# A linear-attention and mixture-of-experts kernel on one core: the experts work on blocks of 256 tokens instead of 512, one unit is a whole expert, and they start three steps behind the attention instead of five

## The chip, the cores and the metric

The kernel runs on one core of a Trainium2 chip. Its time is the device time of one execution in microseconds (us); three runs of the kernel before gave 826.29 to 827.23, with a median of 827.23. The engines are called PE (TensorE, the matmuls), DVE (VectorE), ACT (ScalarE), POOL (GpSimd) and SP (SyncE, which issues most transfers).

## The reference

The input x has 4096 tokens of 256 channels. Two blocks follow each other, each with a layer norm before it and a residual add behind it.

```python
x = x + attn(layernorm(x), w_qkv, w_out)
x = x + ffn(layernorm(x), Wg, Wu, Wd, Wr, temperature)
# attn: 16 heads of 16; q, k get rope, then elu(. * SCALE) + 1
#   kv += outer(k_t, v_t); ks += k_t                 (causal running sums)
#   out_t = (q_t . kv) / max(q_t . ks, 1e-6);  then out @ w_out
# ffn: inh = sigmoid(x @ Wr / temperature); w from the distance of inh to 1/e,
#   with a fallback to the two nearest experts; normalised over 8 experts
#   out = sum_e w_e * ((silu(x @ Wg_e) * (x @ Wu_e)) @ Wd_e)   (256 -> 256 -> 256)
```

All 8 experts are computed for every token; the router gives only their weights.

## The kernel before

The tokens are cut into 32 tiles of 128. Attention goes tile by tile: `qkv`, rope, `scores` (with a causal mask), `av` (scores times v, plus the running state times q), `state`, then the transpose `o_T`, the output projection `proj`, the second layer norm, the transpose `x2_T` and the router's `logit`. The experts go by blocks of B = 512 tokens, which are 4 tiles. A unit is half an expert (128 of its 256 inner channels) for one block. It is `gate` and `up` (six matmuls each with 512 columns moving, line 394), `silu` (ACT, line 615), `h_up` (DVE, line 988), the split of the product into a high and a low part (`h_hi` on ACT, line 622; `h_lo` on POOL, line 1131), and `down` (twelve matmuls with 256 columns moving, line 427). Behind every second unit four `acc` instructions (DVE, line 1000) add the weighted result to the tile's residual. There are 16 units to a block, 8 blocks and so 128 units.

All matrices are kept as a high and a low part in the fp32r type, so each product takes three matmuls (high x high, low x high, high x low). The expert weights are split at the start too: 24 slabs (Wg, Wu and Wd of 8 experts), each loaded by a transfer into a ring of three buffers, rounded on ACT (`slab_hi`, line 479), and its low part made on POOL or DVE (`slab_lo`, lines 1041 and 696).

The order on every engine is written out by hand, instruction by instruction. Each engine runs its own list strictly in order, and a wait stops all that stands behind it. The lists have a head, and then a loop over steps s. In step s the attention takes tile a = s at its front (`qkv`, `scores`) and tile c = s - 1 at its back (`av` to `x2_T`), and four units n = 4 (s - 5) and up are worked. The number 5 is LAG: no unit starts before four tiles are through the attention, since a block has four tiles. Step 5 is the first of the loop, and the first `gate` stands at its start. Attention ends with step 32; steps 33 to 37 hold experts only. The router (28 small DVE instructions, lines 880 to 981, and three on ACT) works on a whole block and stands in every fourth step. Two kinds of ACT function take turns in a step, which costs table loads (line 615 and line 511).

The PSUM banks: gate and up have one each, `down` writes y0 and y1 (two tiles each), the attention has four.

Of the kernel before, what the change touches and what calls it, by code (L numbers as in the profile page):

```python
# [8 lines left out]
F32R = mybir.dt.float32r  # L9
# [17 lines left out]
UNITS = E * KI  # L27
# [41 lines left out]
def build(nc, x, xT, w_qkv, w_out, Wg, Wu, Wd, Wr, temperature, tab, out):  # L69
# [8 lines left out]
    with ctx:  # L78
# [170 lines left out]
        def tensor_program(pe):  # L249
# [140 lines left out]
            def three(ps, weights, b, e_, m_):  # L390
                n = 0
                for wi, xi in ((0, 0), (1, 0), (0, 1)):
                    for k in range(KD):
                        m = pe.matmul(ps, weights[wi][:, e_, k, m_ * P:(m_ + 1) * P], x2[xi][:, b % 2, k, :],  # L394
                                      start=(n == 0), stop=(n == 3 * KD - 1))
                        n += 1
                return m

            def gate(n):
                if not live_unit(n):  # L400
                    return
                b, u = divmod(n, UNITS)
                w.wait_ge(*slab_lo_done(3 * (u // KI)))
                w.wait_ge(s_x2lo, NT * (b + 1))
                w.wait_ge(s_g, n)
                three(G[:, :], wg_p, b, u // KI, u % KI).then_inc(s_gate, 1)

            def up(n):
                if not live_unit(n):
                    return  # L410
                b, u = divmod(n, UNITS)
                w.wait_ge(*slab_lo_done(3 * (u // KI) + 1))
                w.wait_ge(s_h, n)
                w.wait_ge(s_lg, NT)
                three(U[:, :], wu_p, b, u // KI, u % KI).then_inc(s_up, 1)

            def down(n):
                if not live_unit(n):
                    return
                u = n % UNITS  # L420
                w.wait_ge(*slab_lo_done(3 * (u // KI) + 2))
                w.wait_ge(s_hlo, n + 1)
                for t in range(NT):
                    if n % KI == 0 and t % 2 == 0:
                        w.wait_ge(s_acc, NT * (n // KI) - 2 + t)
# [9 lines left out]
            qkv(0); qkv(1); scores(0, 0); scores(0, 1); qkv(2); av(0); scores(1, 0); state(0); qkv(3); scores(1, 1)  # L435
            o_T(0); proj(0); av(1); scores(2, 0); state(1); x2_T(0); o_T(1); scores(2, 1); qkv(4); proj(1); av(2)
            logit(0); state(2); scores(3, 0); x2_T(1); o_T(2); scores(3, 1); logit(1); proj(2); av(3); x2_T(2)
            o_T(3); state(3); proj(3); scores(4, 0); logit(2); x2_T(3); scores(4, 1); logit(3)
            for s in range(LAG, STEPS):
                a, c, d, n = s, s - 1, s - 2, NT * (s - LAG)  # L440
                if s > LAG:
                    logit(d)
                gate(n); qkv(a); up(n); down(n - 2); av(c); gate(n + 1); up(n + 1); down(n - 1); state(c); o_T(c)
                gate(n + 2); proj(c); up(n + 2); down(n); gate(n + 3); scores(a, 0); x2_T(c); up(n + 3); down(n + 1)
                scores(a, 1)

        def scalar_program(act):
# [14 lines left out]
            def load_slab(n):  # L462
# [5 lines left out]
                elif n:  # L468
# [4 lines left out]
            def slab_hi(n):  # L473
# [6 lines left out]
                load_slab(n + NSL - 1)  # L480
# [94 lines left out]
            def x2_hi(g):  # L575
# [3 lines left out]
                w.wait_ge(s_up, UNITS * (b - 1))  # L579
# [49 lines left out]
            a_hi(1, 0); v_copy(2); exp(2); s1(0); a_hi(1, 1); q_hi(2); k_hi(2); slab_hi(6); s2(0); a_hi(1, 2)
            o_hi(0); a_hi(1, 3); x_hi(4); v1(2); qk_copy(3); v2(2); a_hi(2, 0); v_copy(3); wr_hi(); exp(3); s1(1)  # L630
            x2_hi(0); v1(3); a_hi(2, 1); s2(1); q_hi(3); o_hi(1); a_hi(2, 2); v2(3); x_hi(5); slab_hi(7); a_hi(2, 3)
            k_hi(3); qk_copy(4); slab_hi(8); slab_hi(9); v_copy(4); lg_copy(0); s1(2); a_hi(3, 0); x2_hi(1)
            a_hi(3, 1); o_hi(2); exp(4); a_hi(3, 2); v1(4); s2(2); lg_copy(1); a_hi(3, 3); k_hi(4); q_hi(4); v2(4)
            slab_hi(10); o_hi(3); x2_hi(2); slab_hi(11); s1(3); lg_copy(2); a_hi(4, 0); x2_hi(3); a_hi(4, 1); s2(3)
            lg_copy(3)
            for s in range(LAG, STEPS):
                a, c, d, n = s, s - 1, s - 2, NT * (s - LAG)
                router = (s - LAG) // NT if (s - LAG) % NT == 0 else -1
                if s > LAG:
                    lg_copy(d)  # L640
                a_hi(c, 2); th(router); slab_hi(slab(s, 0)); a_hi(c, 3); x_hi(a + 1); qk_copy(a); silu(n); v_copy(a)
                h_hi(n - 1); slab_hi(slab(s, 1)); e1(router); fb(router); exp(a); silu(n + 1); q_hi(a); k_hi(a)
                o_hi(c); h_hi(n); slab_hi(slab(s, 2)); h_hi(n + 1); silu(n + 2); v1(a); slab_hi(slab(s, 3)); s1(c)
                h_hi(n + 2); x2_hi(c); a_hi(a, 0); silu(n + 3); a_hi(a, 1); v2(a); s2(c)

        def vector_program(v):
# [343 lines left out]
            def acc(n, t):  # L990
# [3 lines left out]
                b, e_ = n // UNITS, n % UNITS // KI  # L994
# [266 lines left out]
```

## Time and profile before

| | us |
|---|---|
| median of three runs | 827.23 |
| the profiled execution | 828.06 |
| its span, first to last instruction | 826.3 |
| PE busy | 779.8 (94%) |
| DVE busy | 621.2 (75%) |
| POOL busy | 524.5 (63%) |
| ACT busy | 479.1 (58%) |
| chain that ended last: PE's share | 87% |

The profiled execution's time stands 1.7 us above its span. A matmul's own duration in the trace is longer than its share of PE, because matmuls overlap; the distance between the starts of two of them is what one costs. "Granted clock" is the TensorE clock as a share of 2.4 GHz, and has two levels, 0.5 and 1.0.

### The profile page before, as it was taken

How to read it: one execution, taken by the hardware profiler on the slowest of the kernel's cores; microseconds unless marked ns; L12 is line 12 of the kernel's file. 1: busy time of each engine (PE TensorE's matmuls, PEld its weight loads, DVE VectorE, ACT ScalarE, POOL GpSimd, SP SyncE). 2: the span in 40 equal slices, each digit the busy share in tenths (PEclk: the TensorE clock that was granted, in tenths of full speed). 3: DMA queues.
4: the chain of work that ended last, by engine and by line, in shares of the span. 5: the costliest groups of instructions: out<-in, count | busy, mean ns of one | idle time of the engine just before them, and what ended most of it. 6: DMA issues, size and time to landing. Idle time of an engine off the chain costs nothing.

```text
span 826.3 us, 18214 instructions
## 1 busy us (share of the span) xinstructions
PE 779.8 (94%) x6728; PEld 666.8 (81%) x6728; DVE 621.2 (75%) x1562; ACT 479.1 (58%) x910; POOL 524.5 (63%) x569
## 2 busy tenths in 40 slices
PE   5466899999999999999999999999999999999997
PEld 3345678888888888888888888888888888888886
DVE  5677787879877897778877898778977798756333
ACT  3564576757666656666656566666665666634222
POOL 2789677866667666666677666666776666653332
PEclk9555699999999999999999999999999999999999
DMA  5433333211111221110211231111212121100000
GB/s 149 111 67 88 76 82 88 53 38 40 39 34 39 41 66 39 34 41 20 53 40 39 42 65 33 39 18 32 65 40 39 40 52 27 22 6 26 1 1 25
DMA packets 97320, 38.27 MB, mean 46 GB/s; under 512 B 74192, under 2 KB 96976, under 8 KB 97232
## 3 DMA queue, kind: packets, MB, share of 16 engines
q1 hardware_dynamic: 90704, 30.83, 17.5%
q10 hardware_dynamic: 6528, 6.29, 2.7%
q8 instruction: 53, 0.87, 0.4%
q14 instruction: 35, 0.29, 0.1%
HBM read 16.13 MB, written 4.19 MB: 25 GB/s over the span
## 4 chain that ended last, share of the span: by engine, by line
PE 87%; POOL 4%; DVE 4%; ACT 2%; issue 1%; DMA 1%; ACTq 0%; SPq 0%; DVEq 0%; POOLq 0%
PE y L427 21%; PE gate L394 21%; PE up L394 20%; PE front L275 5%; PE back L320 3%; PE front L276 3%; PE back L356 2%; PE back L298 2%; PE back L331 2%; POOL a_lo L1103 2%; PE front L370 1%; PE front L383 1%; PE back L313 1%; PE back L343 1%; POOL rop L1074 1%
## 5 line engine op out<-in xcount | busy, mean ns | idle before, releaser
L1131 POOL TENSOR_TENSOR h_lo<-work,h_hi 128x512 fp32r<-128x512 f32 x128 | 165.5, 1297 | 71.1 <-ACT h_hi L622 71.1
L1103 POOL TENSOR_TENSOR a_lo<-am,a_hi 128x512 f16<-128x512 f32 x120 | 141.1, 1189 | 30.6 <-ACT a_hi L551 30.4
L427 PE MATMUL y<-wd_hi,h_hi 128*128 128x256 f32 x512 | 144.1, 281 | 1.1 <-DVE xa L1000 1.1
L427 PE MATMUL y<-wd_lo,h_hi 128*128 128x256 f32 x512 | 145.0, 283 | 0.0
L427 PE MATMUL y<-wd_hi,h_lo 128*128 128x256 f32 x512 | 143.5, 280 | 0.0
L622 ACT ACTIVATE h_hi<-work 128x512 fp32r<-128x512 f32 x128 | 80.9, 632 | 75.6 <-PE y L427 42.8
L1082 POOL TENSOR_TENSOR k_st<-qk,k_st 128x512 f16<-128x512 f32 x32 | 39.9, 1248 | 132.5 <-ACT k_st L527 132.5
L1000 DVE SCALAR_TENSOR_TENSOR xa<-y,wo,xa 128x256 f32<-128x256 f32 x256 | 111.5, 476 | 8.1 <-PE y L427 8.1
L988 DVE TENSOR_TENSOR work<-work,up 128x512 f32<-128x512 f32 x128 | 87.2, 681 | 34.3 <-PE up L394 32.5
L775 DVE TENSOR_TENSOR am<-back,cmask 128x512 f32<-128x512 f32 x112 | 74.5, 685 | 49.4 <-PE back L298 49.4
L427 PEld LDWEIGHTS y<-wd_hi,h_hi 128*128 128x128 f32 x512 | 96.3, 188 | 6.5 <-issue 1.2
L427 PEld LDWEIGHTS y<-wd_lo,h_hi 128*128 128x128 f32 x512 | 96.0, 188 | 5.2
L427 PEld LDWEIGHTS y<-wd_hi,h_lo 128*128 128x128 f32 x512 | 97.2, 190 | 0.0
L615 ACT ACTIVATE work<-gate 128x512 f32<-128x512 f32 x128 | 75.9, 593 | 35.5 <-PE gate L394 31.1
L551 ACT ACTIVATE a_hi<-am 128x512 f16<-128x512 f32 x120 | 75.4, 628 | 35.0 <-DVE am L775 32.5
L394 PE MATMUL gate<-x_hi,wg_hi 128*128 128x512 f32 x256 | 88.0, 425 | 0.1
L394 PE MATMUL up<-x_hi,wu_hi 128*128 128x512 f32 x256 | 82.2, 402 | 0.5 <-DVE work L988 0.4
L394 PE MATMUL gate<-x_hi,wg_lo 128*128 128x512 f32 x256 | 80.7, 396 | 0.0
L394 PE MATMUL up<-x_hi,wu_lo 128*128 128x512 f32 x256 | 79.9, 393 | 0.0
L394 PE MATMUL gate<-x_lo,wg_hi 128*128 128x512 f32 x256 | 79.8, 393 | 0.0
L394 PE MATMUL up<-x_lo,wu_hi 128*128 128x512 f32 x256 | 79.5, 392 | 0.0
L751 DVE SCALAR_TENSOR_TENSOR rop<-rop 128x512 f32<-128x512 f32 x32 | 48.5, 1515 | 19.3 <-POOL rop L1074 19.2
(182 smaller groups left out, 1757.4 us busy)
## 6 DMA issues: line engine op xcount, KB each, us to landing
xr<-xT SPq DMA_DIRECT2D x32, 128.0 KB, 2.1
xa<-x SPq DMA_DIRECT2D x32, 128.0 KB, 2.5
out<-xa SPq DMA_DIRECT2D x32, 128.0 KB, 1.9
xa<-Wg ACTq DMA_DIRECT2D x8, 256.0 KB, 2.8
work<-Wu ACTq DMA_DIRECT2D x8, 256.0 KB, 2.8
work<-Wd ACTq DMA_DIRECT2D x8, 256.0 KB, 3.0
work<-w_qkv SPq DMA_DIRECT2D x2, 384.0 KB, 3.6
qT<-q_st SPq DMA_TRANSPOSE x32, 3.2
```

The costliest lines, as they stand in the source:

```text
L275: pe.matmul(R0[:, :], lhs, wqkv_p[wi][:, k, 0:2 * D], start=first, stop=last)
L394: m = pe.matmul(ps, weights[wi][:, e_, k, m_ * P:(m_ + 1) * P], x2[xi][:, b % 2, k, :], start=(n == 0), stop=(n == 3 * KD - 1))
L427: m = pe.matmul(Y[t // 2][:, t % 2 * D:(t % 2 + 1) * D], h_p[hi][:, n % 2, t * P:(t + 1) * P], wd_p[wi][:, u // KI, u % KI, :], start=(n % ...
L551: act.activation(a_p[0][:, heads(r), :], am_place(g, r).rearrange("p (h n) -> p h n", h=4), ACT.Copy).then_inc(s_ahi, 1)
L615: act.activation(hb[:, n % 2, :], G[:, :], ACT.Silu).then_inc(s_g, 1)
L622: act.activation(h_p[0][:, n % 2, :], hb[:, n % 2, :], ACT.Copy).then_inc(s_hhi, 1)
L751: v.scalar_tensor_tensor(out=rop[:, :], in0=rop[:, :], scalar=1.0, in1=rop2[:, :], op0=ALU.add, op1=ALU.add).then_inc(s_rope, 1)
L775: v.tensor_tensor(am_place(g, r).rearrange("p (h n) -> p h n", h=4), score_bank(g, r)[:, :].rearrange("p (h n) -> p h n", h=4), bcast(cmas ...
L988: v.tensor_tensor(hb[:, n % 2, :], hb[:, n % 2, :], U[:, :], ALU.mult).then_inc(s_h, 1)
L1000: v.scalar_tensor_tensor(out=xs, in0=Y[t // 2][:, t % 2 * D:(t % 2 + 1) * D], scalar=wo[:, b % 2, t, e_:e_ + 1], in1=xs, op0=ALU.mult, op1 ...
L1103: pool.tensor_tensor(a_p[1][:, heads(r), :], am_place(g, r).rearrange("p (h n) -> p h n", h=4), a_p[0][:, heads(r), :], ALU.subtract).then ...
L1131: pool.tensor_tensor(h_p[1][:, n % 2, :], hb[:, n % 2, :], h_p[0][:, n % 2, :].bitcast(F32), ALU.subtract).then_inc(s_hlo, 1)
```

## The change

- B goes from 512 to 256, so a block has two tiles and there are 16 blocks. A unit is a whole expert for two tiles; a block has 8 units, and the whole still has 128, four to a step.
- `gate` and `up` write both halves of the expert into one bank: twelve matmuls with 256 columns moving, instead of six with 512. `down` keeps its twelve, and alternates between y0 and y1 from unit to unit. Two `acc` follow every unit, instead of four every second.
- The router stands in every second step instead of every fourth, and works on two tiles.
- LAG goes from 5 to 3. The loop still starts with s = 5 (FULL), but now with unit 8: units 0 to 7 are woven into the written-out head, and all 24 slabs are split there, through a ring of six buffers, alternately on POOL and DVE. Steps 33 to 35 hold experts only.
- All five lists are written in a new order.

```diff
-B = 512
+B = 256
-UNITS = E * KI
+BW = KI * B
+UPS = E // NT
-LAG = 5
+LAG = 3
+FULL = LAG + 2
-NSL = 3
+NSL = 6
...
-            def three(ps, weights, b, e_, m_):
-                n = 0
-                for wi, xi in ((0, 0), (1, 0), (0, 1)):
-                    for k in range(KD):
-                        m = pe.matmul(ps, weights[wi][:, e_, k, m_ * P:(m_ + 1) * P], x2[xi][:, b % 2, k, :],
...
+            def both_halves(ps, weights, b, e_):
+
+                for m_ in range(KI):
+                    for wi, xi in ((0, 0), (1, 0), (0, 1)):
+                        for k in range(KD):
+                            m = pe.matmul(ps[:, m_ * B:(m_ + 1) * B], weights[wi][:, e_, k, m_ * P:(m_ + 1) * P],
+                                          x2[xi][:, b % 2, k, :], start=(m_ == 0 and k == 0 and (wi, xi) == (0, 0)),
...
             def down(n):
...
+                w.wait_ge(s_acc, NT * (n - 1))
                 for t in range(NT):
...
+                    for m_ in range(KI):
+                        tok = slice(m_ * B + t * P, m_ * B + (t + 1) * P)
+                        for wi, hi in ((0, 0), (1, 0), (0, 1)):
+                            m = pe.matmul(Y[n % 2][:, t * D:(t + 1) * D], h_p[hi][:, n % 2, tok], wd_p[wi][:, e_, m_, :],
...
-            for s in range(LAG, STEPS):
-                a, c, d, n = s, s - 1, s - 2, NT * (s - LAG)
-                if s > LAG:
-                    logit(d)
-                gate(n); qkv(a); up(n); down(n - 2); av(c); gate(n + 1); up(n + 1); down(n - 1); state(c); o_T(c)
-                gate(n + 2); proj(c); up(n + 2); down(n); gate(n + 3); scores(a, 0); x2_T(c); up(n + 3); down(n + 1)
-                scores(a, 1)
+            for s in range(FULL, STEPS):
+                a, c, d, n = s, s - 1, s - 2, UPS * (s - LAG)
+                logit(d); gate(n); up(n); qkv(a); down(n - 2); av(c); down(n - 1); gate(n + 1); up(n + 1); o_T(c)
+                state(c); gate(n + 2); proj(c); up(n + 2); down(n); gate(n + 3); up(n + 3); scores(a, 0); x2_T(c)
+                down(n + 1); scores(a, 1)
```

Three places show what moved. The first is PE in the head, around the first gate matmul. Before, it stands behind the scores of tile 4 (`back<-qT,kT`) and the last logits of the first block (`up<-wr_s`), and the qkv of tile 5 follows.

```order
L370 MATMUL up<-ident,nat 128x128 x2
L298 MATMUL back<-qT,kT 128x128 x8
L383 MATMUL up<-wr_s,x_hi 128x16 x2
L386 MATMUL up<-wr_s,x_lo 128x8 x2
L394 MATMUL gate<-x_hi,wg_hi 128x512 x2
L394 MATMUL gate<-x_hi,wg_lo 128x512 x2
L394 MATMUL gate<-x_lo,wg_hi 128x512 x2
L275 MATMUL front<-wqkv_hi,xo_hi 128x512
```

Now it stands behind the scores of tile 2, and gate and up are made of pieces with 256 columns.

```order
L293 MATMUL back<-qT,kT 128x128 x8
L365 MATMUL up<-ident,nat 128x128 x2
L378 MATMUL up<-wr_s,x_hi 128x16 x2
L381 MATMUL up<-wr_s,x_lo 128x8 x2
L293 MATMUL back<-qT,kT 128x128 x8
L390 MATMUL gate<-x_hi,wg_hi 128x256 x2
L390 MATMUL gate<-x_hi,wg_lo 128x256 x2
L390 MATMUL gate<-x_lo,wg_hi 128x256 x2
L390 MATMUL gate<-x_hi,wg_hi 128x256 x2
```

The first unit comes two tiles earlier. The second place is PE in a step of the loop, from the end of `av` (`back<-vx,a_lo`) on. Before, gate and up follow, then (left out behind the last row) `down`, `state` and `o_T`.

```order
L320 MATMUL back<-vx,a_lo 128x51
L394 MATMUL gate<-x_hi,wg_hi 128x512 x2
L394 MATMUL gate<-x_hi,wg_lo 128x512 x2
L394 MATMUL gate<-x_lo,wg_hi 128x512 x2
L394 MATMUL up<-x_hi,wu_hi 128x512 x2
L394 MATMUL up<-x_hi,wu_lo 128x512 x2
L394 MATMUL up<-x_lo,wu_hi 128x512 x2
```

Now `down`, gate and up follow `av`, and the rows from that up on are these, with `o_T` (`back<-ident,nat`) ahead of `state` (`back<-vx,k_st`).

```order
L390 MATMUL up<-x_hi,wu_hi 128x256 x2
L390 MATMUL up<-x_hi,wu_lo 128x256 x2
L390 MATMUL up<-x_lo,wu_hi 128x256 x2
L390 MATMUL up<-x_hi,wu_hi 128x256 x2
L390 MATMUL up<-x_hi,wu_lo 128x256 x2
L390 MATMUL up<-x_lo,wu_hi 128x256 x2
L338 MATMUL back<-ident,nat 128x128 x2
L326 MATMUL back<-vx,k_st 128x34 x24
L390 MATMUL gate<-x_hi,wg_hi 128x256 x2
```

`state` no longer stands between `down` and `o_T`. The third place is DVE in a step with a router, from the denominators (`den`) to the normed output that `o_T` waits for (`nat<-osb,rec`). Before:

```order
L805 TENSOR_SCALAR den<-osb 128x16
L917 SCALAR_TENSOR_TENSOR r_c<-r_eq,iota 128x32
L920 TENSOR_REDUCE q_ws<-r_w 128x4
L922 TENSOR_REDUCE q_ix<-r_c 128x4
L924 TENSOR_SCALAR q_no<-q_ws 128x4
L759 SCALAR_TENSOR_TENSOR qk<-rop 128x512
L930 TENSOR_TENSOR r_s<-iota,q_ix 128x32
L932 SCALAR_TENSOR_TENSOR r_nd<-r_s,r_dist 128x32
L935 TENSOR_REDUCE q_m<-r_nd 128x4
L937 TENSOR_TENSOR r_fw<-r_fb,q_no 128x32
L811 RECIPROCAL rec<-den 128x16
L943 TENSOR_TENSOR r_eq<-r_nd,q_m 128x32
```

Now:

```order
L801 TENSOR_SCALAR den<-osb 128x16
L699 TENSOR_TENSOR xo_lo<-xr,xo_hi 128x256
L755 SCALAR_TENSOR_TENSOR qk<-rop 128x512
L807 RECIPROCAL rec<-den 128x16
L913 SCALAR_TENSOR_TENSOR r_c<-r_eq,iota 128x16
L916 TENSOR_REDUCE q_ws<-r_w 128x2
L918 TENSOR_REDUCE q_ix<-r_c 128x2
L920 TENSOR_SCALAR q_no<-q_ws 128x2
L815 SCALAR_TENSOR_TENSOR nat<-osb,rec 128x256
```

Four of the router's instructions stand between the reciprocal and the normed output now, and the split of the next x tile (`xo_lo`) has come in ahead of them; six of the router's (four before `rec`, and two between it and `nat`) have gone behind `nat`.

## Rows read from the trace of the kernel before

**Rows 1.** The page's slices: busy tenths, and the granted clock.
```profile
PE   5466899999999999999999999999999999999997
...
PEclk9555699999999999999999999999999999999999
```

**Rows 2.** Stretches: length, busy time of PE, PEld, DVE, ACT, POOL, clock, DMA.
```profile
20.00:92.40 72.40, 44.66 (x472) 34.83 (x471) 52.35 (x120) 38.39 (x84) 57.40 (x61) 0.57 0.41 92
92.40:135.00 42.60, 40.25 (x346) 33.18 (x347) 35.95 (x95) 30.84 (x57) 30.21 (x31) 0.96 0.29 74
212.70:588.60 375.90, 375.90 (x3362) 324.81 (x3362) 303.10 (x769) 235.65 (x444) 248.35 (x273) 1.00 0.19 41
```

**Rows 3.** PE in order of time, first gate: start, us, line, operation.
```profile
92.40 1.20 PE L394 MATMUL gate<-x_hi,wg_hi 128*128 128x512 f32 x2
...
95.11 0.63 PE L275 MATMUL front<-wqkv_hi,xo_hi 128*128 128x512 f32 x1
```

**Rows 4.** PE in order of time, one unit behind the attention's end.
```profile
761.74 0.28 PE L427 MATMUL y<-wd_hi,h_hi 128*128 128x256 f32 x1
...
763.17 0.62 PE L394 MATMUL gate<-x_hi,wg_hi 128*128 128x512 f32 x2
...
764.56 0.62 PE L394 MATMUL up<-x_hi,wu_hi 128*128 128x512 f32 x2
...
765.94 0.28 PE L427 MATMUL y<-wd_hi,h_hi 128*128 128x256 f32 x1
```

**Rows 5.** PE in order of time, `proj` and the `up` behind it.
```profile
321.12 0.40 PE L356 MATMUL back<-wout_hi,ox_hi 128*128 128x256 f32 x2
...
321.82 0.62 PE L394 MATMUL up<-x_hi,wu_hi 128*128 128x512 f32 x2
```

**Rows 6.** PE, the first gate of two steps that follow each other.
```profile
306.96 0.72 PE L394 MATMUL gate<-x_hi,wg_hi 128*128 128x512 f32 x2
...
330.44 0.71 PE L394 MATMUL gate<-x_hi,wg_hi 128*128 128x512 f32 x2
```

**Rows 7.** DVE in order of time, head: `x1_add` and `x2_lo` of tile 1.
```profile
65.16 0.43 DVE L834 TENSOR_TENSOR xa<-y,xa 128x256 f32<-128x256 f32 x1 [3.07 <-PE y L356]
...
73.85 0.41 DVE L872 TENSOR_TENSOR x_lo<-up,x_hi 128x256 fp32r<-128x256 f32 x1
```

**Rows 8.** Groups from 212.7 to 588.6 us: count, busy, mean ns, idle before.
```profile
L1000 DVE SCALAR_TENSOR_TENSOR xa<-y,wo,xa 128x256 f32<-128x256 f32 x128 | 56.2, 476 | 0.0
L988 DVE TENSOR_TENSOR work<-work,up 128x512 f32<-128x512 f32 x64 | 43.5, 680 | 0.0
...
L917 DVE SCALAR_TENSOR_TENSOR r_c<-r_eq,iota 128x32 f32<-128x32 f32 x4 | 0.7, 182 | 0.0
...
L615 ACT ACT_TABLE_LOAD x16 | 20.5, 1283 | 10.9 <-PE gate L394 10.9
...
L1131 POOL TENSOR_TENSOR h_lo<-work,h_hi 128x512 fp32r<-128x512 f32 x64 | 82.1, 1287 | 8.9 <-ACT h_hi L622 8.9
```

**Rows 9.** One `slab_lo` on DVE and one on POOL, in order of time.
```profile
28.52 0.68 DVE L696 TENSOR_TENSOR wd_lo<-work,wd_hi 128x512 fp32r<-128x512 f32 x1
...
37.52 1.28 POOL L1041 TENSOR_TENSOR wg_lo<-xa,wg_hi 128x512 fp32r<-128x512 f32 x1
```

**Rows 10.** PE, the gate behind `av`: a step with a router, one without.
```profile
291.00 0.71 PE L394 MATMUL gate<-x_hi,wg_hi 128*128 128x512 f32 x2
...
314.57 0.71 PE L394 MATMUL gate<-x_hi,wg_hi 128*128 128x512 f32 x2
```

**Rows 11.** DVE, the normed output in both, and rope in the second.
```profile
295.19 0.42 DVE L819 SCALAR_TENSOR_TENSOR nat<-osb,rec 128x256 f32<-128x256 f32 x1
...
313.17 1.66 DVE L751 SCALAR_TENSOR_TENSOR rop<-rop 128x512 f32<-128x512 f32 x1 [0.65 <-POOL rop L1074]
...
317.49 0.42 DVE L819 SCALAR_TENSOR_TENSOR nat<-osb,rec 128x256 f32<-128x256 f32 x1
```

**Rows 12.** DVE, the last `acc` instructions.
```profile
822.14 1.66 DVE L1000 SCALAR_TENSOR_TENSOR xa<-y,wo,xa 128x256 f32<-128x256 f32 x4 [2.52 <-PE y L427]
```

More of the change, by code:

```diff
@@ L431, in down @@
                 m.then_inc(s_down, 1)
             colmean()
[L435 to L438, printed above, removed]
@@ new lines, in tensor_program @@
+            proj(0); av(1); state(1); x2_T(0); o_T(1); logit(0); proj(1); qkv(3); scores(2, 0); x2_T(1); logit(1)
+            scores(2, 1); gate(0); up(0); av(2); gate(1); up(1); gate(2); state(2); o_T(2); up(2); proj(2); down(0)
+            gate(3); down(1); up(3); x2_T(2); scores(3, 0); gate(4); logit(2); scores(3, 1); qkv(4); up(4); down(2)
+            gate(5); av(3); up(5); down(3); state(3); gate(6); o_T(3); down(4); proj(3); up(6); gate(7)
+            scores(4, 0); up(7); x2_T(3); down(5); scores(4, 1)
@@ L629, in scalar_program @@
[L629 to L637, printed above, removed]
-                router = (s - LAG) // NT if (s - LAG) % NT == 0 else -1
[L639 to L644, printed above, removed]
+            x_hi(0); load_slab(0); load_slab(1); load_slab(2); load_slab(3); wqkv_hi(0); wqkv_hi(1)
@@ L1020, in vector_program @@
[L1020 to L1031 removed]
+            tcos_scale(0); bn(3); wout_lo(); rtemp_half(); cos(0); rope(0); x_lo(1); x_lo(2); phi(0); slab_lo(1)
@@ new lines, in vector_program @@
+            mean_var2(2); var_eps2(2); slab_lo(15); bn(5); route_both(0); x_lo(4); ln2(2); tcos_scale(4)
+            route_out(0); mask(3, 0); x2_lo(2); mask(3, 1); acc(0, 0); h_up(3); slab_lo(17); mask(3, 2); slab_lo(19)
+            acc(0, 1); acc(1, 0); mask(3, 3); acc(1, 1); h_up(4); cos(4); rope(4); o_sum(3, 0); phi(4); acc(2, 0)
+            o_sum(3, 1); den_max(3); den_rec(3); acc(2, 1); norm(3); x_lo(5); q_lo(4); mean_var(5); acc(3, 0)
+            var_eps(5); o_lo(3); h_up(5); st_add(3); acc(3, 1); x1_add(3); acc(4, 0); slab_lo(21); bn2(3); h_up(6)
@@ new lines, in vector_program @@
+            mean_var2(3); var_eps2(3); mask(4, 0); ln2(3); acc(4, 1); mask(4, 1); h_up(7); x2_lo(3); slab_lo(23)
+            for s in range(FULL, STEPS):
+                a, c, d, n = s, s - 1, s - 2, UPS * (s - LAG)
+                router = (s - LAG) // NT if (s - LAG) % NT == 0 else -1
+                mask(c, 2); acc(n - 3, 0); acc(n - 3, 1); bn(a + 1); mask(c, 3); mean_var(a + 1); h_up(n)
+                route_sum(router); tcos_scale(a); route_zone(router); cos(a); route_nearest(router); var_eps(a + 1)
+                acc(n - 2, 0); o_sum(c, 0); rope(a); o_sum(c, 1); route_weight(router); den_max(c); x_lo(a + 1)
+                phi(a); den_rec(c); route_first(router); norm(c); route_second(router); q_lo(a); o_lo(c)
+                h_up(n + 1); acc(n - 2, 1); acc(n - 1, 0); route_tie(router); route_ix2(router); st_add(c)
+                route_s2(router); x1_add(c); route_both(router); bn2(c); h_up(n + 2); mean_var2(c); var_eps2(c)
+                acc(n - 1, 1); route_out(router); ln2(c); acc(n, 0); mask(a, 0); mask(a, 1); x2_lo(c); acc(n, 1)
+                h_up(n + 3)
@@ new lines, in gpsimd_program @@
+            a_lo(3, 0); a_lo(3, 1); a_lo(3, 2); sin(4, 1); sin(4, 0); a_lo(3, 3); h_lo(3); slab_lo(18); h_lo(4)
+            k_lo(4); slab_lo(20); slab_lo(22); st_rest(3); v_rest(4); h_lo(5); rstd2_pow(3); rstd1_pow(5); s3(3)
+            h_lo(6); v3(4); a_lo(4, 0); a_lo(4, 1)
+            for s in range(FULL, STEPS):
+                a, c, n = s, s - 1, UPS * (s - LAG)
+                h_lo(n - 1); a_lo(c, 2); a_lo(c, 3); sin(a, 1); sin(a, 0); v_rest(a); h_lo(n); k_lo(a); h_lo(n + 1)
+                st_rest(c); rstd2_pow(c); rstd1_pow(a + 1); v3(a); h_lo(n + 2); s3(c); a_lo(a, 0); a_lo(a, 1)
@@ L1207, in sync_program @@
             load_xr(0); load_xa(0); load_xr(1)
-            for g in range(1, NT):
+            for g in range(1, AHEAD + 1):
                 load_xa(g)
```

150 lines of the change are left out of this document (68 added, 82 removed).

## The prediction

> **What bounds the kernel now.** I read the slices first. PE is at 9 tenths from the sixth slice to the last but one; only the first five, about 100 us, show it at 4 to 8 tenths and its clock at half [rows 1]. The stretches say it sharper: from 212.7 to 588.6 us PE is busy for all 375.9 us at clock 1.00, while DVE has 303.1, POOL 248.4 and ACT 235.7; from 20 to 92.4 us PE is busy for only 44.7 of 72.4 us, at a mean clock of 0.57 [rows 2]. So there are two regimes. In the loop the kernel is as long as its matmuls, and only a change in what PE has to do, or a new wait of PE, moves the time. In the head, PE waits for the chain of one tile after the other, and whatever PE work is put there is cheap.
>
> Then the order of time on PE. The first gate starts at 92.40 [rows 3]. A step of the loop takes 330.44 - 306.96 = 23.48 us [rows 6]. A unit costs 765.94 - 761.74 = 4.20 us: 1.43 for `down`, 1.39 for gate, 1.38 for up [rows 4]. Four units are 16.8 us, so the attention's share of a step is 6.7 us. All of PE's work at the full clock is 128 x 4.20 + 32 x 6.7 = 752 us. The span is 826.3; the 74 us between are the head's loss, but for some 11 behind 92.4.
>
> **The split of gate and up: +6 us (+4 to +12).** 256 matmul groups (128 gates, 128 ups) change from 6 x 512 to 12 x 256 columns; that is 3072 columns each time, but 1536 more matmuls in all. The nearest rows with 256 columns are two. `down` is twelve of them in 1.43 us, against (1.39 + 1.38) / 2 = 1.385 for six of 512 [rows 4]: 0.045 x 256 = +11.5 us. `proj` is six of them in 321.82 - 321.12 = 0.70 us [rows 5], so twelve in 1.40: 0.015 x 256 = +3.8 us. Both are of the same type with a new stationary operand each time. Which is nearer is open: gate is like `proj` in that activations that were ready long ago are read, like `down` in its number. I take +6, nearer to `proj`, and keep both ends. Nothing hides this: PE has no idle time in the loop.
>
> The Trainium skill ("TensorE: Matmul & The Clock Gate", section "Wait — 56ns, not 53.3ns?") states a fixed cost of about 2.5 ns for every matmul at the full clock. By that rule the 1536 additional ones would be an estimated +3.8 us. This trace agrees with it in one of two rows: `proj` gives the same, `down` three times as much.
>
> **The head: -11.2 us (-21 to 0).** Eight gates, eight ups and six downs now stand in the head: 16 x 1.385 + 6 x 1.43 = 30.8 us of full-clock PE work that the loop no longer has. I ask when the loop starts now, against 92.4.
>
> Where does the first gate start? It needs `x2_lo` of tile 1, which was at 73.85 + 0.41 = 74.3. Before it DVE waited 3.07 us for `proj(1)`, which stood behind `qkv(4)` [rows 7]; this qkv now stands far behind. Rope, masks and state of tiles 3 and 4, which shared DVE with tile 1's second norm between 65 and 74 us, also come later. Against it, `qkv(2)` is queued behind `av(0)` and `state(0)` now, and more slabs are split early. I take 67 us for the first gate, between 62 and 73.
>
> What stands from there to the loop? On PE the 30.8 us and the rest of the attention's head. That rest is `av`, `state`, `o_T`, `proj` and `x2_T` of tiles 2 and 3, `scores` of 3 and 4, `qkv(4)`, one logit: 1.5 tiles, 10.4 us. So 41.2 us at full clock. The other engines are as full. Against the head of before, DVE gets eight more `slab_lo` at 0.68, eight `h_up` at 0.68, ten `acc` at 0.48 [rows 8, 9], and 28 router instructions at 0.18: 5.4 + 5.4 + 4.8 + 5.0 = 21 us. POOL gets seven `h_lo` at 1.29 and four more `slab_lo` at 1.28: 14 us. ACT gets twelve more `slab_hi`, eight `silu` and seven `h_hi`, all taken at the 0.68 of a DVE instruction of that size, and five table loads at 1.28 [rows 8]: 25 us. The consecutive instructions overlap by some 0.1 us each, so these are upper ends. DVE was busy 52.4 of 72.4 us there, POOL 57.4, ACT 38.4 [rows 2]; with the attention's own work in the window I count about 40 us on DVE, 40 on POOL, 37 on ACT. Four lists of 40 us each, tied together by waits, do not run in 41. In the loop DVE is at 303.1 / 375.9 = 81% [rows 2], the highest share of a helper next to a PE without gaps. 40 us at that share are 49 us. The half clock belongs in it: at 92.4 the first gate took 95.11 - 92.40 = 2.71 us instead of 1.39 and then the clock rose [rows 3], so a few us of half clock, not the whole stretch. I take 48 us: the loop starts at 67 + 48 = 115. Bounds: 105 (62 + 43) and 126 (73 + 53).
>
> The head's term is (115 - 92.4) - 30.8 = -8.2. Behind 92.4 the kernel before lost about 3 us more in the first loop steps, 42.60 - 40.25 = 2.35 idle and 1.3 at half clock [rows 2, 3], which are inside the 48 now: -11.2.
>
> **The loop's waits: +2 us (0 to +10).** The router's 28 instructions stand in every second step, 14 instead of 7 per step. DVE is busy 81% of 23.48 us, 19.0; another 7 x 0.15 make 20.1 of about 23.6. The mean is fine. What can be late is one place. `o_T` needs the normed output. Before, from the gate behind `av` to the end of it, the trace has 295.61 - 291.00 = 4.6 us in a router step and 317.91 - 314.57 = 3.3 without [rows 10, 11]; gate, up and `down`, 1.39 + 1.38 + 1.43 = 4.2, and `state` 0.6 covered 4.8. Now `down`, gate and up stand between `av` and `o_T`, 4.25 us, without `state`. `qkv` ends 1.4 us nearer to `av` as well, since up was moved ahead of it, so rope and its successors are later against `av`. But six router instructions went behind the norm, 0.6 to 0.9 us. I come out within 0.5 us of the limit in each router step, take 0.15 us for 15 of them, and keep 0.7 x 15 = 10 as the end. Waits for gate's and up's banks are no closer than before: a `silu` or `h_up` has a matmul group of 1.4 us beside it and takes 0.7. `down` has two banks in turn, which loosens `acc`.
>
> **The tail: -0.8 us (-1 to 0).** The last `down` is followed by four `acc` in 1.66 us [rows 12], now two in 0.83. Two attention-free steps fewer change nothing in PE's sum. The slab loads, x loads and stores move 38 MB either way and no PE wait in the loop was for them; nothing for those.
>
> **Sum.** 6 - 11.2 + 2 - 0.8 = -4.0. The profiled execution took 828.06, so it becomes 824.1; the median of the runs shown is 0.83 lower, so the forecast for a median is 827.23 - 4.0 = 823.2. Its own range, with each term inside its nearer half, is 819 to 828.
>
> **Rivals.**
> 1. The head swallows the units whole: loop starts at 105, head term -21, and the split costs 4. -21.2 + 4 + 1 - 0.8 = -17: 810. For it: PE idles 27.7 of 72.4 us [rows 2]. Against: POOL has only 15 us free there, and gets 14.
> 2. The head is as full as its helpers: with the first gate at 73 the loop starts at 126, the term is 33.6 - 30.8 - 3 = -0.2, plus 8 for the split, 2 and -0.8: +9, so 836. For it: 24 slabs and eight units in the window in which three engines already have 40 us each, with ACT changing its table five times. Against: chains that wait leave holes which other work can fill. It decides as soon as the loop starts behind 119: then the change is slower.
> 3. The norm is late in each router step: +10 in place of +2, so 831. The place is `o_T`, DVE the releaser, 0.7 us in each of 15 steps. For it: one group fewer of cover. Against: the six moved instructions; and rope, 1.66 us in the loop [rows 11], has `v_rest` (0.7 us) and not `h_lo` (1.29) beside it on POOL now, and may get shorter.
> 4. It gives nothing because terms meet: the loop starts at 118 and the split costs 7: 827. The order of the slabs can do that, when a gate of unit 3 to 7 waits for its weights.
>
> On rope the Trainium skill has a rule against the change ("SBUF — State Buffer", section "SBUF: two separate sides"): the pair shared by DVE and POOL is an exclusive lock, and the later one waits for a whole instruction. This trace fits it: rope took 1.66 us beside a POOL that was at work. By that rule the head, with more `h_lo` and `slab_lo` on POOL, would stretch DVE's instructions, which is rival 2's time, an estimated 836.
>
> **How the numbers follow.** A measurement of this kernel can tell 0.2%, 1.7 us, from no change. The forecast has 0.42, rival 1 0.15, rival 2 0.20, rival 3 0.12, rival 4 0.11. Of the forecast's own 0.42, 0.33 lie under 825.6, 0.08 within 825.6 to 828.9 and 0.01 above. With rival 1 that is 0.48 for faster; with rival 4 it is 0.19 for no change; with rivals 2 and 3 it is 0.33 for slower. The range runs to rival 1's near side, 812, and takes in rival 2's 836: below 812 and above 836 I leave 2 in 10.
>
> **What would show it.** In the changed profile: gate and up as 12 matmuls with starts 0.117 apart (my +4) or 0.119 (+11.5). The first gate near 67 us and the first gate of unit 8 near 115, with the clock at 1.00 from about 72 on. PE's idle time between 150 us and the end under 8 us, and if not, `o_T` <- DVE nat as its first releaser. A step of 23.7 us. It is wrong if the loop starts behind 119 or before 108, or if a step takes over 24 us.

## The result, and the profile after

The changed kernel takes 830.60 us (median of 22 runs, 828.42 to 832.14) against 827.62 us for the kernel before (22 runs on the same chips, 826.29 to 829.83). The ratio is 1.0032, with a 95% interval of 1.0024 to 1.0040: it is slower, by 0.3%. The forecast was 823.2 us and faster; the measured time lies inside the range and on the wrong side of the sign. The profiled execution took 831.75 us, with a span of 830.0.

The page of the changed kernel, busy time and slices, which answers to [rows 1]:

```profile
PE 785.9 (95%) x8264; PEld 742.3 (89%) x8264; DVE 632.4 (76%) x1790; ACT 491.8 (59%) x938; POOL 512.8 (62%) x565
PE   4558999999999999999999999999999999999998
PEclk7558999999999999999999999999999999999999
```

The low stretch at the start is now four slices long, not five. Its stretches, to be set against [rows 2] (length, busy time of PE, PEld, DVE, ACT, POOL, clock, DMA share, GB/s):

```profile
20.00:69.00 49.00, 28.01 (x256) 21.77 (x256) 35.74 (x72) 25.45 (x54) 33.18 (x35) 0.56 0.49 107
69.00:119.00 50.00, 44.81 (x486) 42.39 (x480) 43.31 (x105) 34.91 (x66) 40.18 (x39) 0.97 0.32 70
241.99:577.50 335.51, 334.62 (x3613) 318.81 (x3613) 262.82 (x771) 209.34 (x399) 213.61 (x239) 1.00 0.20 41
```

The head did nearly what was forecast. The first gate starts at 69.06 us (67 was said) and the gate of unit 8, the loop's first, at 119.04 (115 was said), in order of time on PE:

```profile
69.06 0.39 PE L390 MATMUL gate<-x_hi,wg_hi 128*128 128x256 f32 x1
...
119.04 0.36 PE L390 MATMUL gate<-x_hi,wg_hi 128*128 128x256 f32 x1
```

In the loop PE is idle for less than 1 us of 335 by the third stretch, and the whole list of PE's waits between 150 and 815 us has 1.1 us. Read like that, nothing is wrong there. But two `proj` that follow each other start 301.92 - 277.96 = 23.96 us apart, where a step took 23.48 [rows 6], and this is so in steps with a router and in steps without:

```profile
277.51 0.40 PE L390 MATMUL gate<-x_lo,wg_hi 128*128 128x256 f32 x2
277.96 0.51 PE L351 MATMUL back<-wout_hi,ox_hi 128*128 128x256 f32 x2
278.77 0.40 PE L390 MATMUL up<-x_hi,wu_hi 128*128 128x256 f32 x2
...
301.46 0.40 PE L390 MATMUL gate<-x_lo,wg_hi 128*128 128x256 f32 x2
301.92 0.50 PE L351 MATMUL back<-wout_hi,ox_hi 128*128 128x256 f32 x2
```

The last pair of a gate costs 0.23 to 0.24 us wherever nothing waits. Here `proj` starts 0.45 us behind it, and takes 278.77 - 277.96 = 0.81 us instead of the 0.70 of [rows 5]. So some 0.33 us are lost in each step at `proj`, in pieces that are shorter than a matmul's own duration in the trace. PE counts as busy throughout, and no view of waits names them. Who is late is seen when the engines ahead of one `proj` are laid side by side. ACT first, then DVE and PE, of the step around 324 us:

```profile
322.17 1.28 ACT L611 ACT_TABLE_LOAD   x1 [1.21 <-PE gate L390]
323.46 0.60 ACT L611 ACTIVATE work<-gate 128x512 f32<-128x512 f32 x1
323.96 0.62 ACT L514 ACTIVATE q_st<-qk 128x512 f16<-128x512 f32 x1
324.48 0.62 ACT L618 ACTIVATE h_hi<-work 128x512 fp32r<-128x512 f32 x1
325.00 0.38 ACT L569 ACTIVATE ox_hi<-back 128x256 fp32r<-128x256 f32 x1
...
325.41 0.42 DVE L823 TENSOR_TENSOR ox_lo<-back,ox_hi 128x256 fp32r<-128x256 f32 x1
...
323.34 0.38 PE L338 MATMUL back<-ident,nat 128*128 128x128 f32 x2
...
325.43 0.40 PE L390 MATMUL gate<-x_lo,wg_hi 128*128 128x256 f32 x2
325.89 0.51 PE L351 MATMUL back<-wout_hi,ox_hi 128*128 128x256 f32 x2
```

`o_T` (`back<-ident,nat`) is done by about 323.7, but `o_hi` (`ox_hi`) starts only at 325.00. ACT has had no pause since 322.17. It waited 1.21 us for gate(n + 1); then came the load of silu's table, which stands behind that wait, `silu`, `q_hi`, `h_hi` and `o_hi`, then DVE's `ox_lo`, and `proj` is late. Before, the same chain began at 316.29, and ACT even had to wait for `o_T`, since `down(n - 1)` and `state` stood between `up(n + 1)` and `o_T` on PE (as many instructions of ACT stood ahead of `o_hi`, `k_hi` where now `h_hi` is):

```profile
316.29 1.28 ACT L615 ACT_TABLE_LOAD   x1 [0.70 <-PE gate L394]
...
319.99 0.39 ACT L573 ACTIVATE ox_hi<-back 128x256 fp32r<-128x256 f32 x1 [0.77 <-PE back L343]
```

So there was 0.77 us to spare where there is now none. That was the theory that the experiments had to test. The rival was the one of the prediction's own ledger: that the split of gate and up costs twice what I took.

### The profile page after: what moved, and what is told of

It is laid out like the page before. It is cut to its first block, busy times and chain, and to the rows that moved or that the text cites. A ratio compares the mean times of both kernels' runs of the same rounds, so it can differ in the third digit from the quotient of the medians.

```text
span 830.0 us, 21693 instructions
## 1 busy us (share of the span) xinstructions
PE 785.9 (95%) x8264; PEld 742.3 (89%) x8264; DVE 632.4 (76%) x1790; ACT 491.8 (59%) x938; POOL 512.8 (62%) x565
## 4 chain that ended last, share of the span: by engine, by line
PE 75%; ACT 7%; issue 6%; DVE 5%; POOL 3%; DMA 2%; SPq 0%; POOLq 0%; ACTq 0%; DVEq 0%
PE y L424 21%; PE gate L390 17%; PE up L390 15%; PE front L270 6%; PE back L315 3%; PE back L351 3%; PE front L271 3%; PE back L293 2%; ACT q_st L514 2%; ACT h_hi L618 2%; DMA kT<-k_st 2%; POOL a_lo L1104 2%; DVE ox_lo L823 1%; PE front L365 1%; ACT work L611 1%
## 5 line engine op out<-in xcount | busy, mean ns | idle before, releaser
L996 DVE SCALAR_TENSOR_TENSOR xa<-y,wo,xa 128x256 f32<-128x256 f32 x256 | 116.3, 476 | 5.1 <-PE y L424 4.9
L390 PE MATMUL gate<-x_hi,wg_hi 128*128 128x256 f32 x512 | 107.4, 291 | 1.5 <-DVE wg_lo L692 0.9
L390 PE MATMUL up<-x_hi,wu_hi 128*128 128x256 f32 x512 | 102.4, 281 | 0.0
L390 PE MATMUL gate<-x_lo,wg_hi 128*128 128x256 f32 x512 | 102.0, 280 | 0.0
L390 PE MATMUL up<-x_hi,wu_lo 128*128 128x256 f32 x512 | 101.9, 280 | 0.0
L390 PE MATMUL gate<-x_hi,wg_lo 128*128 128x256 f32 x512 | 101.9, 280 | 0.0
L390 PE MATMUL up<-x_lo,wu_hi 128*128 128x256 f32 x512 | 101.8, 280 | 0.0
L771 DVE TENSOR_TENSOR am<-back,cmask 128x512 f32<-128x512 f32 x120 | 79.9, 684 | 24.7 <-PE back L293 15.6
L547 ACT ACTIVATE a_hi<-am 128x512 f16<-128x512 f32 x124 | 77.1, 631 | 23.8 <-DVE am L771 21.9
L390 PEld LDWEIGHTS gate<-x_hi,wg_hi 128*128 128x128 f32 x512 | 78.1, 189 | 2.2 <-DVE wg_lo L692 1.1
L390 PEld LDWEIGHTS up<-x_hi,wu_hi 128*128 128x128 f32 x512 | 78.7, 189 | 0.2
```

Of the source, the lines that this page charges most:

```text
L390: m = pe.matmul(ps[:, m_ * B:(m_ + 1) * B], weights[wi][:, e_, k, m_ * P:(m_ + 1) * P], x2[xi][:, b % 2, k, :], start=(m_ == 0 and k == 0 ...
L547: act.activation(a_p[0][:, heads(r), :], am_place(g, r).rearrange("p (h n) -> p h n", h=4), ACT.Copy).then_inc(s_ahi, 1)
L771: v.tensor_tensor(am_place(g, r).rearrange("p (h n) -> p h n", h=4), score_bank(g, r)[:, :].rearrange("p (h n) -> p h n", h=4), bcast(cmas ...
L996: v.scalar_tensor_tensor(out=xs, in0=Y[n % 2][:, t * D:(t + 1) * D], scalar=wo[:, b % 2, t, e_:e_ + 1], in1=xs, op0=ALU.mult, op1=ALU.add) ...
```

## The experiments

Times are medians; the ratio is to the kernel before on the same chip, with its interval. Its medians were 827.47 to 827.80.

**The split alone.** Before, with each gate and up as twelve matmuls of 256 columns; nothing else.

```diff
-for wi, xi in ((0, 0), (1, 0), (0, 1)):
-    for k in range(KD):
-        pe.matmul(ps, weights..., x2[xi][:, b % 2, k, :])
+for half in range(2):
+    cols = slice(half * 256, half * 256 + 256)
+    for wi, xi in ((0, 0), (1, 0), (0, 1)):
+        for k in range(KD):
+            pe.matmul(ps[:, cols], weights..., x2[xi][:, b % 2, k, cols])
```

> The kernel before, with nothing changed but gate and up: each 512-column matmul is two of 256 columns, the first half of the tokens for all six products, then the second. The result is the reference's. Theory (the split is the dearer part of the change than I took): twelve pieces take 1.41 us as in the changed kernel's trace, against 1.385, and the step grows by 8 x 0.03 = 0.25 us or a little more, so the kernel is 7 to 9 us slower, about 835. Rival (pieces cost what down cost before, 1.43): +11.5, about 839. Rival (the split is nearly free in this order, and the changed kernel's 0.49 us per step are its waits): under +4, below 831.

834.98 us, ratio 1.0084 (1.0065 to 1.0103): +7.0 us by the ratio, against the +6 of the prediction. The step is 23.70 to 23.79 us, 23.74 in the mean. The split explains half of what a step got longer (23.48 to 23.96), not all.

**The split with each weight used twice in a row.** The same, with the loop over the halves innermost, so that two successive matmuls have the same stationary operand.

> As the split alone, but the two pieces of 256 columns with the same weights follow each other, so half of the matmuls have the weights of the one before. If the cost is one per matmul, whatever its weights are, it equals the split alone within 1 us. If it hangs on new weights, it is some 4 us or more below it.

834.56 us, ratio 1.0079 (1.0060 to 1.0098): the same. The cost hangs on the number of matmuls, not on how often the stationary operand is a new one; the trace has a weight load for each of these matmuls here too, so what a load left out would give is not shown.

**`o_hi` ahead of `h_hi` on ACT.** The changed kernel, with two instructions of the ACT list swapped.

```diff
-silu(n + 1); q_hi(a); h_hi(n); o_hi(c); k_hi(a)
+silu(n + 1); q_hi(a); o_hi(c); h_hi(n); k_hi(a)
```

> The changed kernel, with one swap on ACT in the loop: o_hi(c) ahead of h_hi(n). In the changed kernel's trace h_hi (0.52) runs at 324.48, o_hi at 325.00, o_lo on DVE at 325.41, and proj, which waits for o_lo, starts 0.45 us behind the last matmul of gate instead of 0.23, and is 0.11 longer. Theory (the loop's 0.49 us per step are about half the split and half this wait): proj is no longer late, a step takes 23.65 to 23.75 instead of 23.97, and the kernel gains 6 to 9 us, to 822 to 825. Rival (all is the split): the step stays at 23.9 or more, no gain. Rival (the wait moves on: h_lo is 0.4 later and down or gate waits for it): the step gets no shorter or longer.

831.79 us, ratio 1.0050 (1.0035 to 1.0064): no gain, and my expectation missed. `proj` now starts 324.47 - 324.21 = 0.26 us behind the last pair of the gate, so the gap ahead of it is nearly gone; yet it still takes 325.29 - 324.47 = 0.82 us. The excess is in its first pair, 0.34 us to the next where the other two have 0.24. `proj` waits for `ox_lo`, which DVE ended at 324.42, so it still started on the last of its inputs:

```profile
324.21 0.40 PE L390 MATMUL gate<-x_lo,wg_hi 128*128 128x256 f32 x2
324.47 0.51 PE L351 MATMUL back<-wout_hi,ox_hi 128*128 128x256 f32 x2
324.81 0.40 PE L351 MATMUL back<-wout_lo,ox_hi 128*128 128x256 f32 x2
325.05 0.40 PE L351 MATMUL back<-wout_hi,ox_lo 128*128 128x256 f32 x2
325.29 0.28 PE L390 MATMUL up<-x_hi,wu_hi 128*128 128x256 f32 x1
```

And a wait has appeared that the changed kernel did not have, behind it (waits of PE, 150 to 815 us; total, times, longest):

```profile
PE up L390 <- DVE work L984: 2.6, 13, 0.2
```

All of them stand in steps with a router. From `proj` to `proj`, a step without one now takes 23.8 us, nearly what the theory had, and one with a router 24.2; the mean is 24.0, as without the swap. What makes the router steps long is seen on POOL and DVE, first with the swap, then in the changed kernel:

```profile
325.55 1.19 POOL L1083 TENSOR_TENSOR k_st<-qk,k_st 128x512 f16<-128x512 f32 x1
325.72 1.05 DVE L939 TENSOR_TENSOR r_eq<-r_nd,q_m 128x16 f32<-128x16 f32 x1
329.17 0.67 DVE L984 TENSOR_TENSOR work<-work,up 128x512 f32<-128x512 f32 x1
```

```profile
326.49 1.17 POOL L1083 TENSOR_TENSOR k_st<-qk,k_st 128x512 f16<-128x512 f32 x1
327.13 0.57 DVE L939 TENSOR_TENSOR r_eq<-r_nd,q_m 128x16 f32<-128x16 f32 x1
330.11 0.67 DVE L984 TENSOR_TENSOR work<-work,up 128x512 f32<-128x512 f32 x1
```

The router's small `r_eq` ends 0.03 us behind POOL's `k_st` in both. With `h_hi` later on ACT, POOL's `h_lo` and `k_st` come 0.47 us later against DVE's list, and `r_eq` takes 1.05 us instead of 0.57. `h_up` (`work<-work,up`) then ends at 329.84, and `up`, which could start at 328.11 + 1.41 = 329.52 behind its gate, waits for it. So the swap took 0.2 us of the 0.36 away in each step, and lost some 0.45 in every second one at a place that had hardly more slack.

**The table load ahead of the wait.** The changed kernel, with a one-column Silu on a constant in front of `silu(n + 1)`. It needs nothing from PE, so it draws the table load ahead of the wait for gate(n + 1).

```diff
+dum = sb("dum", [P, 1])
+def silu_set():
+    w.wait_ge(s_mone, 1)
+    act.activation(dum[:, :], mone[:, :], ACT.Silu)
-fb(router); silu(n + 1); q_hi(a)
+fb(router); silu_set(); silu(n + 1); q_hi(a)
```

> The changed kernel, with a one-column silu on ACT put behind the router's exps in the loop, so that the table is loaded there and not after the wait for gate, where the trace has it at 322.17, 1.28 us, ahead of silu, q_hi, h_hi and o_hi. Theory (proj waits for this chain in every step): the chain is 1.2 us earlier, the wait goes, a step takes 23.65 to 23.75, the kernel 822 to 825, as with the swap. Rival (all is the split): no gain.

819.62 us, ratio 0.9899 (0.9876 to 0.9922): 11 us less than the changed kernel, and 1% faster than the kernel before. ACT, in order of time: the load follows its predecessor at once, and `silu` starts 0.11 us behind the one-column instruction:

```profile
316.73 1.28 ACT L616 ACT_TABLE_LOAD   x1
318.02 0.20 ACT L616 ACTIVATE dum<-mone 128x1 f32<-128x1 f32 x1
318.13 0.58 ACT L612 ACTIVATE work<-gate 128x512 f32<-128x512 f32 x1
...
319.65 0.37 ACT L570 ACTIVATE ox_hi<-back 128x256 fp32r<-128x256 f32 x1
```

`proj` starts right behind the gate, as before the change, and a step takes 23.61 us:

```profile
321.18 0.40 PE L391 MATMUL gate<-x_lo,wg_hi 128*128 128x256 f32 x2
321.41 0.39 PE L352 MATMUL back<-wout_hi,ox_hi 128*128 128x256 f32 x2
...
322.10 0.40 PE L391 MATMUL up<-x_hi,wu_hi 128*128 128x256 f32 x2
```

The groups of silu's table loads between 241.99 and 577.5 us of the changed kernel, and between 238 and 580 us of this one, show the same in a line each (count, busy, mean ns, idle before):

```profile
L611 ACT ACT_TABLE_LOAD x14 | 18.0, 1283 | 17.5 <-PE gate L390 17.5
```

```profile
L616 ACT ACT_TABLE_LOAD x15 | 19.2, 1283 | 0.3
```

One load a step in both (the second window is 6.5 us longer), each as long; only the idle time in front of each is gone.

**No table loads at all.** The changed kernel with Exp in place of Silu, so that ACT keeps one table. The experts' activation function is another one here.

```diff
-act.activation(hb[:, n % 2, :], G[:, :], ACT.Silu)
+act.activation(hb[:, n % 2, :], G[:, :], ACT.Exp)
```

> The changed kernel with exp in the place of silu in all 128 units, so that every activation is in one table set and ACT loads none; the expert's nonlinearity is another one, so its output is not the reference's. Theory (proj waits for o_lo at the end of a chain on ACT that begins with a table load behind the wait for gate): the chain is gone with the load, and the step is that of the early table, 23.61 us; the kernel is at 818 to 820, perhaps 1 to 3 us lower still since the head's loads go too. Rival (ACT as a whole is too full in the head and the loop, 2 loads of 1.28 us a step): clearly below the early table, under 814.

818.70 us, ratio 0.9881 (0.9857 to 0.9905). This is within 1 us of the early load, and the step is 23.6 us in both. So the two loads of a step cost next to nothing as work; all their price was the place of one of them.

**The same one-column Silu in the kernel before.** A control: there the chain had 0.77 us to spare.

```diff
-exp(a); silu(n + 1); q_hi(a)
+exp(a); silu_set(); silu(n + 1); q_hi(a)
```

> Control: the kernel before with the same one-column silu at the same place. Theory: before the change proj did not wait (its gate took 1.47 and proj 0.70, no longer than the unhindered ones), so nothing is gained, 827 to 828. Rival (the early table is an improvement of its own that has nothing to do with the change): some 5 to 10 us less.

828.43 us, ratio 1.0006 (0.9988 to 1.0025), in ten runs: nothing. It is not a saving that any kernel of this kind would get; it takes back a wait that the change brought.

**`down(n - 1)` back behind `up(n + 1)`.** The changed kernel, with nothing done on ACT, but with the cover on PE that the order before had.

```diff
-av(c); down(n - 1); gate(n + 1); up(n + 1); o_T(c)
+av(c); gate(n + 1); up(n + 1); down(n - 1); o_T(c)
```

> The changed kernel with one thing undone on PE: down(n - 1) stands again behind gate(n + 1) and up(n + 1), as in the kernel before, and not ahead of them. Theory: gate(n + 1) ends 1.4 us earlier against o_T and proj, so the chain table load, silu, q_hi, h_hi, o_hi, o_lo is done before proj in time, the step is 23.6 to 23.7 and the kernel 818 to 823. Rival (the early table helps in another way, through h_lo or exp): the step stays above 23.8. Rival (av's results or h_hi then come later for others): a new wait of PE, no gain.

820.06 us, ratio 0.9894 (0.9873 to 0.9916). One entry of PE's list moved by two places gives back 10.5 us, nearly the same, and the step is 23.62 us. The load still stands behind the wait for the gate in ACT's list, but that gate is early enough now, and the load starts 322.37 - 317.67 = 4.70 us ahead of `proj` here, where it was 325.89 - 322.17 = 3.72 in the changed kernel and 321.12 - 316.29 = 4.83 before. ACT and PE of this kernel:

```profile
317.67 1.28 ACT L611 ACT_TABLE_LOAD   x1
```

```profile
322.14 0.40 PE L390 MATMUL gate<-x_lo,wg_hi 128*128 128x256 f32 x2
322.37 0.40 PE L351 MATMUL back<-wout_hi,ox_hi 128*128 128x256 f32 x2
```

**Both mends.** The early load and the moved `down`.

> The changed kernel with the early table and with down(n - 1) behind up(n + 1). Theory (both take away the same wait of proj, and the loop is then as long as its matmuls): nothing more than either alone, 818 to 821, step 23.6. Rival (each takes away a wait of its own): 5 us or more below them, under 815.

819.72 us, ratio 0.9911 (0.9894 to 0.9927): no more than either alone, as one chain with one slack wants it.

**Early loads in the head too.** The early-load kernel, with the one-column Silu at three more places of the head.

```diff
-v1(3); th(0); ... e1(0); exp(3)
+v1(3); silu_set(); th(0); ... e1(0); exp(3); silu_set()
-a_hi(3, 3); exp(4)
+a_hi(3, 3); exp(4); silu_set()
```

> The changed kernel with the early table load in the loop and, three times, in the written-out head. Theory (in the head PE waits for chains through all engines, of which the table loads are only one): 0 to 2 us below the early table in the loop alone, 817.5 to 820. Rival (ACT's five table loads hold up the head): 4 us or more below it.

820.52 us, ratio 0.9904 (0.9882 to 0.9927): nothing. In the head the loads are not what PE waits for.

**A second load on the chain.** The changed kernel, with a one-column Exp right behind `silu(n + 1)`, which puts another table change ahead of `q_hi`, `h_hi` and `o_hi`. It is the dose turned up.

```diff
-silu(n + 1); q_hi(a)
+silu(n + 1); exp_set(); q_hi(a)
```

> The changed kernel with a one-column exp on ACT between silu(n + 1) and q_hi, so that another table load of 1.28 us stands in the chain to o_lo, and a third one returns to silu behind it. Theory (the chain decides in every step): proj is another 1.3 us or a little more late, the step is 25.2 to 25.5 us instead of 23.97, the kernel 865 to 880. Rival (table loads are covered, and the wait comes from elsewhere): under 840.

872.19 us, ratio 1.0542 (1.0521 to 1.0564). A step is 337.61 - 312.15 = 25.46 us, 1.5 longer than in the changed kernel: one load of 1.28 us and one instruction of 0.20. With that dose the wait is long enough for the trace to name it. PE's two `proj` in order of time, and the waits of PE from 150 to 850 us:

```profile
312.15 0.51 PE L352 MATMUL back<-wout_hi,ox_hi 128*128 128x256 f32 x2 [1.57 <-DVE ox_lo L828]
...
337.61 0.51 PE L352 MATMUL back<-wout_hi,ox_hi 128*128 128x256 f32 x2 [1.57 <-DVE ox_lo L828]
```

```profile
PE back L352 <- DVE ox_lo L828: 40.7, 26, 1.6
```

The whole of the added ACT time arrives on PE, in 26 steps. So in the changed kernel the chain had no slack left, which is what the theory said.

## Why the prediction was wrong

The start of `proj` of tiles 6 and 30 divides a span at the same place of the work. The starts in the changed kernel, and in the one with the early load:

```profile
182.09 0.51 PE L351 MATMUL back<-wout_hi,ox_hi 128*128 128x256 f32 x2
...
757.39 0.51 PE L351 MATMUL back<-wout_hi,ox_hi 128*128 128x256 f32 x2
```

```profile
179.73 0.39 PE L352 MATMUL back<-wout_hi,ox_hi 128*128 128x256 f32 x2
...
746.45 0.39 PE L352 MATMUL back<-wout_hi,ox_hi 128*128 128x256 f32 x2
```

| us, by spans | before | split alone | early load | after |
|---|---|---|---|---|
| start to `proj` of tile 6 | 156.6 | 156.2 | 179.7 | 182.1 |
| 24 steps to `proj` of tile 30 | 564.2 | 569.7 | 566.7 | 575.3 |
| from there to the end | 105.5 | 106.8 | 71.3 | 72.6 |
| span | 826.3 | 832.8 | 817.7 | 830.0 |

- **The split, +6: right.** Alone it measured +7.0 by the ratio of the medians (5.4 to 8.5 by its interval) and +6.5 in the span. Its starts are 0.118 apart, between the two rows that bounded it. The Trainium skill's 2.5 ns for each matmul ("TensorE: Matmul & The Clock Gate", section "Wait — 56ns, not 53.3ns?") would give +3.8; measured it is 7.0 / 1536 = 4.6 ns for each additional one, so the rule falls short here and the measurement decides.
- **The head, -11.2, and the tail, -0.8: right in size, the head in part by luck.** Set the early load against the split alone, so that neither the split nor the chain is in it, and count the 8 units that are done earlier at 4.2 us each, 33.6 in all. Up to tile 6 it is 179.7 - 156.2 - 33.6 = -10.1, and behind tile 30 it is 71.3 - 106.8 + 33.6 = -1.9: -12.0 together, as forecast. But two misses cancel in it. The loop started 4 us later than I said (119.04 for 115; 118.23 with the early load). And the kernel before lost 6.0 us behind 92.4, twice what I took (the row below). With these two numbers the term is (118.2 - 92.4) - 30.8 - 6.0 = -11.0.
- **The order of the blocks: a term that I had not.** The 24 steps take 3.0 us less with the early load than with the split alone (566.7 against 569.7). It is not `down`, although behind the attention one takes 1.40 us now (805.84 - 804.44, the unit below) and 1.43 before [rows 4]: counted from its first matmul to the next block's, the 96 `down` of these steps take 143.5 us with the early load and 142.5 with the split alone. The 96 gates take 139.7 against 144.4. A gate between a `down` and an `up` takes 1.41 us, and one behind `logit`, `av`, `o_T` or `state`, or ahead of `scores`, 1.50 or 1.51; the new order has two of the first kind in a step, the split alone none. Why a block is dearer there was not tested.
- **The loop's waits, +2: the step that failed.** The step put the danger at `o_T`, waiting for DVE's norm, in router steps only, and took 0.15 us for 15 of them, with an end of +10. Measured, the wait is at `proj`, for `ox_lo` at the end of ACT's chain, in every step, 0.36 us each (575.3 - 566.7 = 8.6 in 24 steps). With what lies outside these it is 830.0 - 817.7 = 12.3 by spans and 11.0 by medians. I had asked what DVE does between `av` and `o_T` and found it just in time, and it was: no wait for `nat` is in the trace behind the head. I did not follow ACT's list over the same piece of the program, though the same lost cover of `down(n - 1)` bears on it, and though [rows 8] show silu's table loads idle for `gate` 10.9 us in 16 times before the change. That row said that the load begins only when the gate is done, so that its 1.28 us belong to the chain.

The 6.0 us are worked out like this. The second loop step of the kernel before starts with this gate:

```profile
117.78 0.71 PE L394 MATMUL gate<-x_hi,wg_hi 128*128 128x512 f32 x2
```

The first loop step took 117.78 - 92.40 = 25.38 us although it has no `down(n - 2)` and `down(n - 1)` yet, some 3.0 us of work that a later step has. From 92.40 to `proj` of tile 6 it was 156.64 - 92.40 = 64.2 us. Two later steps and the piece up to their `proj` are 47.0 + 14.2 us, and less these 3.0 they are 58.2.

Without the term of the loop's waits the sum would be 6 - 11.2 - 0.8 and the measured sum is 6.5 - 3 - 12 = -8.5, which is the early-load kernel. With it, the change turns from 1% faster to 0.3% slower. Rival 3 had the price (+10, 831) by another place; that it met the measured 830.6 is luck. Rival 1, the empty head, and rival 2, the full one at 126, fall with the start at 119.04. Rival 4 had both of its conditions nearly met (a loop start at 118, a split of 7) and gave 827; without the wait at `proj` the kernel is at 819.6, since the head saved more than that sum says.

A unit behind the attention, where nothing waits for ACT's table, has the forecast's prices: gate 1.42, up 1.41, `down` 1.40, in all 4.23 against 4.20 [rows 4]:

```profile
801.61 0.40 PE L390 MATMUL gate<-x_hi,wg_hi 128*128 128x256 f32 x2
...
803.03 0.40 PE L390 MATMUL up<-x_hi,wu_hi 128*128 128x256 f32 x2
...
804.44 0.28 PE L424 MATMUL y<-wd_hi,h_hi 128*128 128x256 f32 x1
...
805.84 0.39 PE L390 MATMUL gate<-x_hi,wg_hi 128*128 128x256 f32 x2
```

Of the signs that I named: the starts are 0.118 apart (said 0.117 or 0.119); the first gate and the loop's start were 2 and 4 us late, and 119.04 is just behind the 119 at which I would have called the prediction wrong and the change slower. That sign spoke for the wrong reason: with the early load the loop starts at 118.23, with `down` moved at 119.09, and both kernels are 1% faster than before. Also, the full clock came from 66.8 us, but fell again to half from 77.0 to 80.4; PE's idle time behind 150 is under 8 us, as said, and this sign was worthless, since it does not see the waits that decided; a step is 23.96, under the 24 at which I would have called the prediction wrong, and 0.26 over the 23.7 said. I set that threshold too far: 0.3 us in each of 28 steps is already more than twice the forecast's gain.

## What to carry to other kernels

When work is reordered on the busiest engine, take each other engine's list over the same stretch and add it up from the wait that holds its first entry, table loads included: a load stands behind its activation's wait, and a one-column activation of the same function ahead of that wait moves it out of the chain. If a helper had slack at a point only because some block stood there, moving the block spends that slack for all helpers, not only the one that was looked at. And on an engine whose instructions overlap, losses of 0.1 to 0.3 us show neither as idle time nor as waits; compare the distance of two equal starts, step by step, or turn the suspected cost up until the trace names it.

## What the runs showed of the hardware

- A gate or up as twelve matmuls of 256 columns instead of six of 512 costs 4.6 ns for each additional matmul (7.0 us for 1536, 3.5 to 5.5 ns by the interval), and about the same (0.79% of the time for 0.84%) when two in a row share their stationary operand.
- A table load took 1283 ns each time, and an activation behind it that waited for nothing else started 0.01 us after it. The Trainium skill ("ScalarE: Activation LUTs", section "What ACT_TABLE_LOAD costs") states the 1283 ns, which the trace bears out, and some 1380 ns of draining besides, which no load here shows.
- A `proj` that starts on the last of its inputs loses more than the gap ahead of it: its first pair takes 0.34 us (324.81 - 324.47, with `o_hi` first) where the next pairs take 0.24, and in all it takes 0.82 instead of 0.70.
- An instruction on DVE can last as long as one on POOL does. The router's `r_eq` at line 939 (944 with the early load; 128x16) ended 0.03 us behind POOL's `k_st` in each of 12 steps of three kernels (changed, early load, `o_hi` first), and took 0.57 or 1.05 us by how early in `k_st` it began; the last one of the early-load kernel, at 786.76, has no instruction of POOL beside it and took 0.16.
